# Sixteen turns written out one by one: new orders on every engine and a PSUM bank for each job and turn

## The reference

```python
delta = softplus(einsum('blr,er->ble', delta, W_dt) + b_dt)
dA = exp(delta[..., None] * A)
dBx = (delta * x)[..., None] * Bm[:, :, None, :]
_, hs = associative_scan(combine, (dA, dBx), axis=1)
y = einsum('blen,bln->ble', hs, Cm) + Dp * x
```

## Time and profile before

| | us |
|---|---|
| median of 3 runs | 776.01 (769.16 to 778.88) |
| the profiled execution | 778.98 |
| its span | 777.2 |
| PE busy | 677.7 (87%) |
| DVE busy | 617.4 (79%) |
| ACT busy | 524.6 (67%) |
| POOL busy | 331.9 (43%) |

### The profile page before, as it was taken

How to read it: one execution, slowest core, us unless ns; L and a number is a source line. 1 busy time by engine, 2 the same in 40 slices (tenths; PEclk the granted TensorE clock), 3 DMA queues, 4 the chain that set the end, 5 groups by cost and what they waited for, 6 DMA issues and landing times.

```text
span 777.2 us, 18707 instructions
## 1 busy us (share of the span) xinstructions
PE 677.7 (87%) x7686; PEld 317.6 (41%) x7686; DVE 617.4 (79%) x1082; ACT 524.6 (67%) x930; POOL 331.9 (43%) x291
## 2 busy tenths in 40 slices
PE   4766689899999999999999998999999997988774
PEld 2322234344444444444444453444444433433321
DVE  6899889789898989898989898987888986755230
ACT  1442476858788787878687968677786848575631
...
PEclk9985899999999999999999999999999999999875
...
GB/s 76 74 83 49 49 46 31 25 32 56 22 54 32 47 40 32 56 24 63 16 71 14 73 2 73 43 26 44 48 19 37 9 1 36 7 8 4 5 6 26
...
## 3 DMA queue, kind: packets, MB, share of 16 engines
...
...
## 4 chain that ended last, share of the span: by engine, by line
PE 65%; DVE 14%; ACT 11%; issue 4%; DMA 2%; SPq 2%; POOL 1%; DVEq 0%; ACTq 0%
PE ring L1004 19%; ACT pm L837 7%; PE ring L1074 6%; PE ring L1061 5%; PE ring L1160 4%; PE ring L1132 3%; PE ring L1011 3%; PE ring L1015 3%; PE ring L1036 3%; PE ring L1141 2%; PE ring L977 2%; PE ring L1123 2%; PE ring L1029 2%; PE ring L1098 2%; PE ring L1091 2%
## 5 line engine op out<-in xcount | busy, mean ns | idle before, releaser
L837 ACT ACTIVATE pm<-ring,two_col 93x744 f32<-93x744 f32 x128 | 105.8, 872 | 12.5 <-PE ring L1061 10.9
L1439 DVE TENSOR_TENSOR hidw<-hid,ring 128x744 f32<-128x744 f32 x48 | 44.4, 926 | 30.0 <-PE ring L1123 22.5
L1061 PE MATMUL ring<-q_exp,qk 32*93 32x372 f32 x512 | 56.4, 509 | 13.2 <-ACT pm L837 8.7
L1074 PE MATMUL ring<-pm,v 97*32 97x93 f32 x2048 | 53.5, 250 | 9.5 <-ACT pm L837 8.8
L693 POOL TENSOR_TENSOR h_in<-base_D,carry_D 128x372 f32<-128x372 f32 x16 | 17.0, 1061 | 102.2 <-DVE base_D L1327 102.2
L689 POOL TENSOR_TENSOR du_A<-delta_A,x_A 128x744 f32<-128x744 f32 x16 | 37.4, 2339 | 50.4 <-ACT delta_A L785 38.9
L872 ACT ACTIVATE hid<-ring,b_col 128x372 f32<-128x372 f32 x96 | 49.1, 563 | 8.2 <-PE ring L1141 8.2
L1074 PEld LDWEIGHTS ring<-pm,v 97*32 97x32 f32 x2048 | 42.3, 112 | 27.6 <-ACT pm L837 19.2
L711 POOL TENSOR_TENSOR q_exp<-qk,mask_q 128x1488 f32<-128x1488 f32 x16 | 42.9, 2682 | 17.6 <-DVE qk L1377 17.4
L879 ACT ACTIVATE hid<-ring,b_col 128x744 f32<-128x744 f32 x48 | 42.2, 878 | 12.0 <-PE ring L1132 7.9
L1132 PE MATMUL ring<-hid,w 64*64 64x372 f32 x384 | 42.8, 517 | 5.8 <-ACT v L829 3.4
...
...
## 6 DMA issues: line engine op xcount, KB each, us to landing
...
```

What stands on the lines that cost most here:

```text
L837: a.activation(pm[q % 2][h][0:TOUT].rearrange("m a j n -> m a (j n)"), out_of(f"att.s{q}{h}")[0:TOUT, :, 0:COLS], ACT.Square, bias=two_col ...
L1061: ins = mm(o[h][0:TOUT, b, 0:COLS], qk[r:r + 32, 1, q * TOUT:(q + 1) * TOUT], q_exp[r:r + 32, q].rearrange("p j n -> p (j n)"), start=True ...
L1074: ins = mm(o[32 * j:32 * j + 32, 0, h * TOUT:h * TOUT + TOUT], rows[:, at:at + 32], pm[q % 2][h][:, b, j, :], start=(b == 0), stop=(b == 1 ...
L1439: tt(hidw[k][:], hid2[:], out_of(f"ffn.g_{k}")[:, :, 0:COLS], ALU.mult).then_inc(me, 1)
```

## The change

`FIRST`, `ORDER` and `LAST` give way to one table for each engine, in which all 16 turns are written out with their turn number. The sets of steps are the same on each engine (901 on PE, 787 on ACT, 711 on DVE, 211 on POOL, 115 on SP). In PE's table a bank, or two for a pair, stands behind each step, so a job can lie in another bank in each turn. The old `BANK` stays, as `SPARE`, for the general version. `out_of`, `qk_made` and their callers get the turn as an argument. No operation, tile or wait rule is changed.

```diff
-        PRE, POST = 6, 3
         ORDER = {
...
+            "pe": ("prep.w0:0/0 prep.w2:0/1 prep.w1:0/2 A.xT:0/4 A.dpre:0/6 B.xT:0/4 prep.qkvp:0/0 B.dpre:0/6 "
+                    "A.z:0/2 A.b:0/4 A.s:0/0 A.c:0/6 B.z:0/2 A.xT:1/4 B.b:0/0 B.s:0/2 A.dpre:1/4 B.c:0/6 B.xT:1/2 "
...
-        BANK = dict([
+        SPARE = dict([
...
-        def entries(text, end=0):
-            return [(w, int(g) + end) for w, g in (entry.split(":") for entry in text.split())]
-
-        def turns(who):
-
-            lags = entries(ORDER[who])
-            return [(w, i - lag) for i in range(PRE, NG - POST) for w, lag in lags if 0 <= i - lag < NG]
-
-        MAIN = {who: entries(FIRST[who]) + turns(who) + entries(LAST[who], NG) for who in ORDER}
+        def entries(text):
+            return [(w, int(g)) for w, g in (entry.split("/")[0].split(":") for entry in text.split())]
+
+        MAIN = {who: entries(ORDER[who]) for who in ORDER}
         for who, steps_ in MAIN.items():
             assert len(set(steps_)) == len(steps_)
-        last_ssm = max(i for i, (w, g) in enumerate(MAIN["dve"]) if w[0] in UNITS)
-        MAIN["dve"].insert(last_ssm + 1, ("prep.flags", NG - 1))
-        MAIN["pe"].insert(MAIN["pe"].index(("ffn.h2_2", NG - 1)), ("prep.flag", NG - 1))
-        MAIN["dve"].insert(MAIN["dve"].index(("ffn.hidw2", NG - 1)), ("prep.again", NG - 1))
         JOBS["prep.flag"] = (1, "dve prep.again")
-        BANK["prep.flag"] = BANK["ffn.rh"]
...
+        BANK = {(w, g): b for w, b in SPARE.items() for g in range(NG, 2 * NG)}
+        for entry in ORDER["pe"].split():
+            step_, banks_ = entry.split("/")
+            w_, g_ = step_.split(":")
+            BANK |= {(job, int(g_)): int(b) for job, b in zip(PAIRED.get(w_, (w_,)), banks_.split(","))}
...
         in_bank = {}
         for step_, g_ in MAIN["pe"] + GENERAL["pe"]:
             for w_ in PAIRED.get(step_, (step_,)):
-                here = range(BANK[w_], BANK[w_] + JOBS[w_][0])
+                here = range(BANK[w_, g_], BANK[w_, g_] + JOBS[w_][0])
                 BEFORE[w_, g_] = {in_bank[b] for b in here if b in in_bank}
                 in_bank.update({b: (w_, g_) for b in here})
...
-        def out_of(job):
-
-            return ring[:, BANK[job]:BANK[job] + JOBS[job][0]]
+        def out_of(job, g):
```

More of the change, by code:

```diff
@@ L510, in waiter @@
             return need
-        def out_of(job):
-            return ring[:, BANK[job]:BANK[job] + JOBS[job][0]]
+        def out_of(job, g):
+            return ring[:, BANK[job, g]:BANK[job, g] + JOBS[job][0]]
         def walk(steps, do, late):
@@ L767, in ssm @@
                     need(g, *x_read(u), back=1)
[L768 removed]
+                    a.activation(xs[u][:, 0:2], out_of(f"{u}.xT", g)[:, :, 0:COLS], ACT.Copy).then_inc(me, 1)
                 if s == "exp":
                     need(g, f"pe {u}.dpre")
[L771 removed]
+                    o = out_of(f"{u}.dpre", g)[:, :, 0:WIDE[u]]
                     if g < NG:
@@ L837, in attention @@
                     a.activation(pm[q % 2][h][0:TOUT].rearrange("m a j n -> m a (j n)"),
-                                 out_of(f"att.s{q}{h}")[0:TOUT, :, 0:COLS], ACT.Square,
+                                 out_of(f"att.s{q}{h}", g)[0:TOUT, :, 0:COLS], ACT.Square,
                                  bias=two_col[0:TOUT], scale=0.5 ** 0.5).then_inc(me, 1)
@@ L843, in attention @@
                     need(g, "pe att.nrow", f"dve att.att{q // 2}", back=1)
-                    a.activation(yT[:, q], out_of(f"att.y{q}")[:, 0, 0:2 * TOUT], ACT.Copy).then_inc(me, 1)
+                    a.activation(yT[:, q], out_of(f"att.y{q}", g)[:, 0, 0:2 * TOUT], ACT.Copy).then_inc(me, 1)
                 if s == "nln":
@@ L847, in attention @@
                     need(g, "pe att.nb0", "pe att.nb1", back=1)
-                    a.activation(y_rec[:], out_of("att.nrow")[:, 0, 0:2 * TOUT], ACT.Ln).then_inc(me, 1)
+                    a.activation(y_rec[:], out_of("att.nrow", g)[:, 0, 0:2 * TOUT], ACT.Ln).then_inc(me, 1)
                 if s == "rec":
@@ L945, in bank @@
                     need(g_e, *JOBS[earlier][1:])
-                return out_of(job)
+                return out_of(job, g)
             def prepare(g, u, s):
@@ L1299, in made_by @@
                     need(g, f"pe {u}.{job}")
-                    return out_of(f"{u}.{job}")[:, :, 0:wide]
+                    return out_of(f"{u}.{job}", g)[:, :, 0:wide]
                 if s == "delta":
@@ L1335, in ssm @@
                     done_before = (g - NG) * (4 * (NS - 1)) + FLAG[u] * (NS - 1)
-                    ob, oc = (out_of(f"{u}.gen")[:, 2 * k:2 * k + 2, 0:wide] for k in range(2))
+                    ob, oc = (out_of(f"{u}.gen", g)[:, 2 * k:2 * k + 2, 0:wide] for k in range(2))
                     q, w = sem("gen_w_steps"), sem("gen_steps")
```

50 lines of the change are left out of this document (22 added, 28 removed), and 509 rows, old and new, of tables (FIRST, LAST, ORDER).

## The result

The changed kernel takes 786.1 us (median; 785.6 to 787.2) beside 772.6 us for the kernel before: ratio 1.020, 95% interval 1.012 to 1.028. Predicted were 782, in a range of 765 to 797. Its profiled execution has a span of 784.6 us, before it was 777.2. The two profiles do not show all of the 13.5 us between the medians: the one after (786.31 us) is an ordinary execution, the one before (778.98) lies 6.4 us over its median, so that the spans are only 7.4 us apart.

A forecast was written before the change was run, and what follows sets the result against it. PE was taken as the bound, DVE close behind and deciding the head. Start of att.cen:0 112 + spacings 593 + last chain 77.7 = 782.7 us span; plus 1.8 less 3 gives 781.5, called 782, range 765 to 797.

The forecast's parts named there:

- Start of att.cen:0: First attention matmul, at 87.75 us before: queue hold and extra DVE work ahead of it move it to 112, +24 us.
- The walk down SyncE's queue: Head: adding up SyncE's loads and swaps in order puts D.swap:0 at 93 and the end of D.based:0 at 112.
- the hold of SyncE: Head: 19 late loads and four x loads ahead of turn 0's swap delay its issue by 14.1 us, to 29.95.
- The spacings: Fifteen intervals from att.cen:0 to att.cen:15: 611.7 us before, 593 after, from work moved out and less idle time.
- turns 2 to 9: Middle: free banks save a third of 1.5 us idle a turn, 0.5 x 8 = 4 us; possibly worse by as much.
- Swap behind four loads: Rival, SyncE: swaps behind four x loads put att.cen:0 at 121 or later, time over 791.5 to about 798; chance 0.25.
- Turns 9 to 15: Late turns: steady pattern lasts two turns longer, gaining 4.5 us; reaching the stretch without filler earlier costs 5.
- Turns 0 to 2: Early attention turns, idle 8.2 + 3.7 us: DVE work done ahead gives back 4 us.
- The work moved out of the spacings: PE: 6.5 us done ahead of att.cen:0 and 4.5 moved behind att.cen:15, 11.0 us less between them.
- The last chain: From att.cen:15 to the end: 4.5 us of moved steps fall into 24.3 us idle, so 77.7 us stays.
- The hidden hold: Rival, head: late loads issue at once, A.swap:0 at most 1 to 5 us late, time 768 to 773; chance 0.10.
- The slow chain on SyncE: Rival, head: loop of swap, z, xT and loads sends D.swap:0 after about 102, time over 791.5; chance 0.25.

The follow-up runs named there:

- a_late_back: Changed kernel with its 38 late weight loads moved back to where the kernel before has them on SyncE and ScalarE: 790.6 us, ratio to before 1.025.
- a_both: Changed kernel with the late weight loads at the old places and the x loads behind the swaps: 773.0 us, ratio to before 0.999.
- a_head_before: Changed kernel with x loads behind the swaps and the old order on all engines up to PE's 50th step: 768.1 us, ratio to before 0.996.
- b_free_banks: Kernel before, order untouched, each job and turn taking the PSUM bank free for longest: 765.3 us, ratio to before 0.994.
- a_load_behind: Changed kernel with the four x loads for the next turn right behind each A and B swap, not ahead: 771.3 us, ratio to before 1.001.
- b_load_ahead: Kernel before with the next turn's four x loads right ahead of the A and B swaps in turns 3 to 13: 800.5 us, ratio 1.037.
- a_apart: a_load_behind with DVE and POOL steps shifted so DVE operations wholly in SBUF avoid running POOL operations, banks given anew: 771.5 us, ratio to before 1.003.
- b_tail_after: b_free_banks with the changed kernel's order on each engine from D.dpre:14 on: 754.1 us, ratio to before 0.978.

## Why the prediction came out

The time lies in the range and its sign is right, with 782 forecast and 786.1 measured; but that is in good part luck. Of the three terms only the first came out, and two of its parts stood for something else; the other two were off in opposite directions. And against the kernel before the loss is 13.5 us, where the prediction has 6. One of its own signs of being wrong came true: from turn 2 to 9 the turns take 44.9 us on the mean and not 40.5. And the last stretch, for which it asked 77 to 79 us, is 72.6. By its own steps:

- **Start of att.cen:0, forecast 112, measured 111.4.** The swap at 32.15 against 29.95, D.swap:0 at 94.4 against 93, A.x:0 at 28.4 against 25.7 (ScalarE's first late load took 3.4 us): as counted. The walk down SyncE's queue matched the trace up to D.swap:0; its end is 1.2 us short, since it counts to the end of D.based:0 and att.cen:0 stood that much behind it before. But the working also added 14.1 us for the hold of SyncE to 12.3 for DVE, and no late load that is moved back down gives its part of the hold back (a_late_back, a_both). Nor is SyncE's queue all of it: with the x loads behind the swaps D.swap:0 goes out at 84.6, 9.8 us earlier, and att.cen:0 comes only 4.1 us earlier. By the runs the 24 us are 4 us for the x loads ahead of the swaps, about 12 for the order of the first 50 steps (107.4 to 95.3; 14 against a_both, which has the late loads at the same places), and 8 to 12 that are left (95.3 in a_head_before against 83.6 to 87.8). That these are the work of A:3 and B:3, for which the prediction had 7 to 12, is argued from the size; no run has it alone.
- **The spacings, forecast 593, measured 600.6.** The step that failed is "turns 2 to 9", where free banks were to win 0.5 us a turn. Banks win nothing there (b_free_banks), and the idle time rose by 13.1 us. "Swap behind four loads" was named only as a rival for att.cen:0; in the steady turns it had a price, "a steady turn 1 us worse", but it was left out of the sum. In the new turn it costs 1.3 us (9.2 us in seven turns, a_load_behind), in the old 2.9 (b_load_ahead). The lock between DVE and POOL was not in the working; it takes 14.6 us of DVE's time there, but a_apart gave half of that back and won nothing.
- **Turns 9 to 15** were sized at 4.5 us of gain less 5; idle time fell by 14.5, about half of it from turn 9 to 13 (10.7 to 3.6) and half from 13 to 15 (10.4 to 2.8). For the second half the last two turns' order is a part of the cause (b_tail_after: 10.1 to 6.4 in the same turns). The first half was not tried.
- **Turns 0 to 2** gave back 3.5 us of idle time, 4 were forecast. The work moved out of the spacings came to 6.3 us on PE (568.1 to 561.8), not 11.0.
- **The last chain, forecast 77.7, measured 72.6.** That the moved steps cost nothing was right. "77.7 stays" was not: norm_rows stands 28.8 us behind att.cen:15 and not 34.0, and from there to the end nothing changed (43.8 and 43.9). Of these 5.2 us free banks give 2.9 (b_free_banks: 31.1), so the bank term was put in the steady turns and belonged here. The other 2.4 come with the new order (28.8 in b_tail_after too).
- **From span to time.** The working took 3 us off, since the profile before stood so far over the median of its three runs. Over the median of 772.6 it stands 6.4, the profile after 0.2 over its own. The spans are 784.6 against 782.7 forecast, the times 786.1 against 782.
- **The rivals.** The hidden hold, which was also the Trainium skill's rule (DMA: Bandwidth & Descriptors, "Issuing engines are not separate DMA queues"), fell by its mechanism: the issues took 5.23 and 2.67 us for six and the swap waited for them. The slow chain on SyncE stopped short of its point (94.4 against 102), but it had the right place and the right queue.

So errors of -0.6 at the start, +7.6 in the spacings and -5.1 in the last chain covered each other, and 782.7 against 784.6 of span says less for the working than it seems.
